# Batch by batch instead of all batches first: where the input norm, the first routing and the filter's hidden layers stand in a two-layer kernel

## What is computed

```python
# layer 0, on normalised tokens x
q, k, v = x @ w_q.T, x @ w_k.T, x @ w_v.T
attn = softmax(causal(rotate(q) @ rotate(k).T / sqrt(128))) @ v      # 4 batches, 1024 x 1024
h = xres + attn
# expert layer 0: 8 experts, capacity 512 each, top-1, routed by xn @ wg
dispatch = one_hot(argmax(logits)) * (place < C)
out0 = combine(gate, dispatch, exp_in @ W[e].T + b)
# layer 1: long convolution; the filter h comes from a small MLP of positions
h = gelu(pos_emb @ W1 + b1); h = gelu(h @ W2 + b2); h = (h @ W3 + b3) * decay
y = ((x @ Wu + bu) * causal_fft_conv(x @ Wv + bv, h)) @ Wo + bo
# expert layer 1: 8 experts, top-2, hidden width 256
```

## Time and profile before

| what | us |
|---|---|
| three runs: median (lowest to highest) | 493.45 (492.63 to 493.60) |
| the profiled execution, whole | 493.04 |
| its span, first to last instruction | 491.2 |
| busy: PE | 366.0 (75%) |
| busy: DVE | 294.4 (60%) |
| busy: POOL | 258.4 (53%) |
| busy: ACT | 225.9 (46%) |

### The profile page before, as it was taken

One profiled execution on the slowest core, in us unless ns is written; L12 is line 12 of the kernel. 1 busy time (PEld: TensorE's weight loads), 2 busy tenths in 40 slices (PEclk: granted clock), 3 DMA queues, 4 the chain that ended last, 5 costly groups with the idle time before them and its releaser, 6 DMA issues.

```text
span 491.2 us, 7805 instructions
## 1 busy us (share of the span) xinstructions
PE 366.0 (75%) x2302; PEld 298.7 (61%) x2302; DVE 294.4 (60%) x782; ACT 225.9 (46%) x551; POOL 258.4 (53%) x254
## 2 busy tenths in 40 slices
PE   2485588869997975949997978898887777766720
PEld 0272255658675644737996867787776667755620
DVE  3977569614773796474688993478438772244105
ACT  1373042325332316334343066434567676687724
POOL 2754766733666323016566676666666555365540
PEclk9999599997998999687998999999999999999975
DMA  9999999823321330001111282445322215422407
GB/s 211 396 197 262 166 140 135 268 51 85 87 75 40 111 89 1 1 5 39 34 34 37 69 261 75 142 140 151 112 69 75 63 29 158 137 74 74 126 11 252
DMA packets 64744, 55.05 MB, mean 112 GB/s; under 512 B 6819, under 2 KB 56683, under 8 KB 64446
## 3 DMA queue, kind: packets, MB, share of 16 engines
q1 hardware_dynamic: 57888, 41.71, 35.6%
q0 software_dynamic: 6656, 12.51, 8.4%
q10 hardware_dynamic: 158, 0.33, 0.4%
HBM read 30.44 MB, written 25.27 MB: 113 GB/s over the span
## 4 chain that ended last, share of the span: by engine, by line
PE 44%; issue 13%; ACT 12%; DVE 10%; DMA 10%; POOL 8%; SPq 1%; ACTq 0%; POOLq 0%; DVEq 0%
PE psS L1161 19%; PE psO L1161 15%; PE psT L1161 7%; ACT hT L1122 7%; POOL slots L826 4%; DMA slots<-row,slot 4%; DMA moe<-ys,xs 2%; POOL w L847 2%; DMA xres<-in_x 2%; ACT row L1027 1%; PE psT L1263 1%; POOL moe L836 1%; DVE work L1713 1%; DVE xres L1747 1%; DMA moe<-ys,ring 1%
## 5 line engine op out<-in xcount | busy, mean ns | idle before, releaser
L813 POOL DMA_INDIRECT slots<-row,slot x64 | 69.3, 1083 | 57.0 <-DVE slot L1580 22.4
L836 POOL DMA_INDIRECT moe<-ys,xs x61 | 61.1, 1001 | 58.3 <-issue 16.6
L1161 PE MATMUL psO<-ring,hT 128*128 128x128 f32 x320 | 45.2, 284 | 45.1 <-ACT hT L1122 45.1
L1161 PEld LDWEIGHTS psO<-ring,hT 128*128 128x128 f32 x320 | 38.7, 191 | 53.4 <-issue 53.4
L1122 ACT ACTIVATE hT<-psT,ring 128x128 f32<-128x128 f32 x160 | 45.6, 368 | 45.7 <-PE psT L1161 45.7
L1868 DVE TENSOR_TENSOR ys<-psO,ring 128x256 f32<-128x256 f32 x40 | 17.0, 424 | 75.3 <-PE psO L1161 75.1
L1055 ACT ACTIVATE ring<-w 128x642 f32 x80 | 55.9, 761 | 1.1 <-issue 1.0
L1161 PE MATMUL psS<-work 128*128 128x512 f32 (+3 forms) x96 | 42.6, 558 | 12.6 <-DVE work L1696 8.8
L836 POOL DMA_INDIRECT moe<-ys,w x35 | 38.0, 1087 | 23.3 <-DVE ys L1868 9.7
L1020 ACT ACTIVATE work<-psT 128x512 f32<-128x512 f32 (+3 forms) x32 | 16.5, 516 | 66.6 <-PE psT L1263 66.6
L826 POOL DMA_INDIRECT slots<-row,slot x32 | 34.9, 1091 | 18.1 <-DMA slots<-row,slot 10.9
(11 more groups left out here) (272 smaller groups left out, 781.4 us busy)
## 6 DMA issues: line engine op xcount, KB each, us to landing
slots<-xs SPq DMA_DIRECT2D x14, 516.0 KB, 14.7
mats<-in_iv SPq DMA_DIRECT2D x16, 256.0 KB, 3.7
xs<-slots SPq DMA_DIRECT2D x61, 64.5 KB, 1.9
w<-in_w SPq DMA_DIRECT2D x8, 321.0 KB
w<-slots SPq DMA_DIRECT2D x35, 64.5 KB, 1.9
xres<-in_x SPq DMA_DIRECT2D x4, 512.0 KB, 9.7
mats<-in_fw SPq DMA_DIRECT2D x1, 2048.0 KB, 11.3
moe<-xs SPq DMA_DIRECT2D x4, 512.0 KB, 7.8
```

Of the source, the lines that this page charges most:

```text
L813: pool.indirect_dma_start(slots1[:, :], bass.IndirectOffsetOnAxis(ap=(slot1, slot2)[k][:, i:i + 1], axis=0), row[:, i, :], None, bounds_ch ...
L836: pool.indirect_dma_start(dst[:, :], bass.IndirectOffsetOnAxis(ap=row_slots[l][m][:, D:ROWW].bitcast(I32), axis=0), ys[:, n % UNROLL, :], ...
L1161: return pe.matmul(o, lhsT, rhs, start=start, stop=stop)
```

## The change

- *Order.* Only batch 0 is normalised, transposed, projected and rotated before row 0. `transpose_tokens(1)` follows `scores(0)`; batches g = 1, 2, 3 get `values_and_gates(g)` in row g - 1, and batches 2 and 3 `transpose_tokens(g)` in row g - 2. DVE normalises batches 0 and 2, ACT batches 1 and 3 (`norm_rows0`, with a bias from `negative_means0`).
- *Filter.* The first hidden layer begins before row 0, its tanh is in row 1, its last polynomial in row 2; the second layer stands in rows 3 to 5. The polynomials leave POOL; DVE does each with one two-input instruction (four in all instead of eight on POOL). The last layer and the spectrum move from rows 2 to 7 to rows 6 to 11, and `filter_layer` uses bank `S[1]` both times.
- *First routing.* Its first six steps are behind row 2 on DVE, the rest at the head of row 3.
- *Later rows.* Expert layer 0 starts in row 12 instead of 8 (`MOE0_FROM`), the split of the biases in row 13 instead of 9; most additions, norms and steps of the second routing move one row later.
- *SP.* q/k weights and rotation tables come ahead of x's later batches; the DFT matrices, the weights of expert layer 0 and the biases come behind the first fill. The weights of layer 1 (2.7 MB) are loaded behind the first 16 sorted tiles instead of ahead of them.

```diff
-FILT_RADIX_AT, FILT_DFT_AT = 3, 6
-SPLIT_AT = 9
-GATES_AT = (24, 25, 29)
-NORM_AT = {23: [(0, 0), (0, 1)], 24: [(1, 0), (1, 1)], 27: [(2, 0)], 28: [(2, 1)]}
-COUNTS_AT = 27
+FILT_HIDDEN_AT, FILT_RADIX_AT, FILT_DFT_AT = 3, 7, 10
+SPLIT_AT = 13
+ROUTING0_AT = 2
+GATES_AT = (25, 26, 29)
+NORM_AT = {24: [(0, 0), (0, 1)], 25: [(1, 0), (1, 1)], 27: [(2, 0)], 28: [(2, 1)]}
+COUNTS_AT = 28
-MOE0_FROM = 8
+MOE0_FROM = 12
-ADD_BEFORE_MAX = {22: (4, 8), 23: (12, 16), 25: (20, 24), 29: (24, 28), 31: (28, 30)}
-ADD_BEHIND_ROW = {21: (0, 4), 22: (8, 12), 24: (16, 20)}
-ROUTING_BEFORE_MAX = {26: 6, 28: 8}
-ROUTING_BEHIND_ROW = {26: 6, 27: 10, 28: R1_STEPS}
+ADD_BEFORE_MAX = {23: (4, 8), 24: (12, 16), 26: (20, 24), 29: (24, 28), 31: (28, 30)}
+ADD_BEHIND_ROW = {22: (0, 4), 23: (8, 12), 25: (16, 20)}
+ROUTING_BEFORE_MAX = {27: 6, 29: 8}
+ROUTING_BEHIND_ROW = {27: 6, 28: 10, 29: R1_STEPS}
...
+def tokens_at(n):
+    return [n + 2] if 0 <= n + 2 < B else []
+def values_at(n):
+    return [n + 1] if 0 <= n + 1 < B else []
...
+            load_x(0)
+            sp.dma_start(cst[:, :], cst_in).then_inc(cst_loaded, 16)
             sp.dma_start(wqk, wqk_in).then_inc(rope_loaded, 16)
+            sp.dma_start(wvg, wvg_in).then_inc(w_a_loaded, 16)
+            load_x(1)
             sp.dma_start(rope, rope_in).then_inc(rope_loaded, 16)
+            load_x(2)
+            load_x(3)
...
 @block.gpsimd
-            inverse_std(0)
-            inverse_std(1)
-            filter_cubic(0)
-            inverse_std(2)
-            inverse_std(3)
-            filter_gelu(0)
-            filter_cubic(1)
-            filter_gelu(1)
+            for g in range(B):
+                inverse_std(g)
...
 @block.scalar
+            take_transposes(0)
+            take_values(0)
+            norm_rows0(1)
+            act.wait_ge(filt_loaded, 32)
+            filter_layer(0)
             exp_rows(0)
+            take_transposes(1)
             for n in range(NT):
                 take_pt(n)
                 if n + 1 < NT:
                     exp_rows(n + 1)
+                for g in values_at(n):
+                    take_values(g)
+                for g in tokens_at(n):
+                    take_transposes(g)
+                if n == 0:
+                    norm_rows0(B - 1)
+                if n == ROUTING0_AT:
+                    routing0_exp()
+                if n == FILT_HIDDEN_AT - 2:
+                    filter_tanh(0)
+                if n == FILT_HIDDEN_AT:
+                    filter_layer(1)
+                if n == FILT_HIDDEN_AT + 1:
+                    filter_tanh(1)
...
 @block.tensor
+            transpose_tokens(0)
+            pe.wait_ge(rope_loaded, 32)
+            pe.wait_ge(tr_free, 1)
+            project(0, 0)
+            pe.wait_ge(w_a_loaded, 16)
+            values_and_gates(0)
             pe.wait_ge(filt_loaded, 32)
             filter_layer(0)
...
             scores(0)
+            transpose_tokens(1)
             for n in range(NT):
                 for b, h in projections_at(n):
                     project(b, h)
                 if n + 1 < NT:
                     scores(n + 1)
+                if n == ROUTING0_AT + 1:
+                    wait_emptied(pe, O_USES, O_AT[("c", 0)])
+                    routing_counts(0, o_bank("c", 0))
+                if n == FILT_HIDDEN_AT:
+                    filter_layer(1)
                 transpose_probs(n)
...
                 if n:
                     weigh_values(n - 1)
+                for g in values_at(n):
+                    values_and_gates(g)
+                for g in tokens_at(n):
+                    transpose_tokens(g)
...
 @block.vector
+            norm_stats(0)
+            norm_rows(0)
+            norm_stats(1)
             dve.wait_ge(rope_loaded, 32)
             rotate(0, 0)
+            negative_means0(1)
+            norm_stats(2)
+            row_max(0)
+            norm_stats(3)
+            norm_rows(2)
...
+                if n == ROUTING0_AT + 1:
+                    finish(first_layer_routing)
+                if n == FILT_HIDDEN_AT - 1:
+                    filter_gelu(0)
+                if n == FILT_HIDDEN_AT + 1:
+                    filter_cubic(1)
+                if n == FILT_HIDDEN_AT + 2:
+                    filter_gelu(1)
...
+                if n == 0:
+                    negative_means0(B - 1)
+                    filter_cubic(0)
+                if n == ROUTING0_AT:
+                    dve.wait_ge(cst_loaded, 16)
+                    dve.wait_ge(vg_free, 4 * B)
+                    take(first_layer_routing, R0_OH)
```

More of the change, by code:

```diff
@@ L526, in two_layer_kernel @@
         issued = sem("issued")
-        T_USES, O_USES = [], []
+        T_USES = [("xt", u) for u in range(4)]
+        O_USES = [("vg", u) for u in range(4)]
         for n in range(NT):
+            if n == ROUTING0_AT + 1:
+                O_USES.append(("c", 0))
             T_USES += [("p", n, c) for c in range((n % J + 4) // 4)]
@@ L538, in two_layer_kernel @@
                 O_USES.append(("o", n - 1))
+            O_USES += [("vg", 4 * g + u) for g in values_at(n) for u in range(4)]
+            T_USES += [("xt", 2 * g + u) for g in tokens_at(n) for u in range(2)]
             T_USES += [("x", e) for e in expert0_at(n)]
@@ L729, in _ @@
             for n in range(TILES0):
+                if n == UNROLL:
+                    sp.wait_ge(rad_f, RAD_F)
                 load_rows(0, slots0, n)
+                if n == RING[0] - 1:
+                    for a, b in [(w12[:, e, :], w12_in[e]) for e in range(E)] + [
+                            (wv[:, :], wv_in), (wu[:, :], wu_in), (wg1[:, :], wg1_in), (wo[:, :], wo_in)]:
+                        sp.dma_start(a, b).then_inc(l1_w_loaded, 16)
             for m in range(RING[0]):
@@ L952, in take_values, with norm_rows0 @@
                                    ACT.Copy).then_inc(vg_free, 1)
+            def norm_rows0(g):
+                act.wait_ge(neg0_done, g // 2 + 1)
+                for i in range(J * g, J * g + J):
+                    act.activation(row[:, i, 0:D], xres[:, i, :], ACT.Identity, bias=nbias[:, i:i + 1],
+                                   scale=rstd[:, i:i + 1]).then_inc(xn0_act, 1)
             def filter_layer(k):
                 act.wait_ge(f_full, k + 1)
-                act.activation(hx[0:FO, :], S[k][0:FO, :, :].rearrange("p a m -> p (a m)"), ACT.Identity,
+                act.activation(hx[0:FO, :], S[1][0:FO, :, :].rearrange("p a m -> p (a m)"), ACT.Identity,
                                bias=(f1b, f2b)[k], scale=(1.0, 0.5)[k]).then_inc(f_act, 1)
@@ L1491, in norm_rows, with negative_means0, filter_cubic, filter_gelu @@
                     ts(row[:, i, 0:D], xres[:, i, :], mv[:, i, 0:1], rstd[:, i:i + 1], ALU.subtract,
-                       ALU.mult).then_inc(xn_done, 1)
-            def norms(k0):
-                norm_stats(k0)
-                for k in range(k0 + 1, k0 + B):
-                    norm_stats(k)
-                    norm_rows(k - 1)
-                norm_rows(k0 + B - 1)
+                       ALU.mult).then_inc(xn0_dve if k < B else xn_done, 1)
+            def negative_means0(g):
+                tiles = slice(J * g, J * g + J)
+                dve.wait_ge(rstd_done, J * (g + 1))
+                stt(nbias[:, tiles], mv[:, tiles, 0], -1.0, rstd[:, tiles], ALU.mult, ALU.mult).then_inc(neg0_done, 1)
+            def filter_cubic(k):
+                dve.wait_ge(f_act, 3 * k + 2)
+                stt(ht[0:FO, :], ht[0:FO, :], 1.0, hx[0:FO, :], ALU.add, ALU.mult).then_inc(f_dve, 1)
+            def filter_gelu(k):
+                dve.wait_ge(f_act, 3 * k + 3)
+                stt(hg[0:FO, :], hg[0:FO, :], 1.0, hx[0:FO, :], ALU.add, ALU.mult).then_inc(f_dve, 1)
             n_rt = [0]
@@ L1539, in routing0 @@
                 yield from inverse_sum(None, NT, gate0[:, :])
-                yield from earlier_tokens(0, None, NT, O[0])
+                yield from earlier_tokens(0, None, NT, o_bank("c", 0))
                 assert n_rt[0] == R0_CUM
```

127 lines of the change are left out of this document (45 added, 82 removed).

## The result

The changed kernel takes **500.76 us** (median of four, 500.17 to 501.10) against 493.04 us (491.58 to 493.60) for the kernel before on the same chip: ratio 1.016, 95% interval 1.0134 to 1.0185. The profiled execution took 500.60 us for a span of 498.5, 7.3 us more than the 491.2 before. The forecast was 498.4 us, slower.

The account below looks back on a forecast made before the run. One chain of scatter, send-back, additions, routing and second scatter, headed by `slot0`, was taken to bound the kernel. 7.2 + 2.3 - 1.0 - 2.9 - 0.6 = +5.0 on 493.45 gives 498.4 us; own range 495.5 to 502, with rivals 489.5 to 503.5.

Parts of the forecast that it names:

- Part 1: Start of row 0: `scores(0)` needs only the rotation tables, comes at about 23.5, row 0 some 30 us earlier.
- Part 2: Start of the first scatter: gates wait behind ScalarE's list of rows 0 to 2; first issue 60.1 against 52.84, +7.2.
- Part 3: Scatter to additions: TensorE waits some 5 us in row 12; second expert falls in a projection row, +2.3.
- idle time in row 12: Sign in row 12: TensorE idle for a sorted tile until 113 to 119; no idle time would show the forecast wrong.
- The supply of the send-back: GpSimd's send-back of expert results: second expert comes in row 14, a projection row of 8.65 against 6.1, +2.3.
- Part 4: First addition to second slots, 46.1 before: one attention row fewer, but routing and exponential behind other work, -1.0.
- Part 5: Second scatter: GpSimd's 2.87 wait for the last tiles' statistics goes, -2.9, and a slack is used up, -0.6.
- the slack of 0.6: At 281, TensorE taking the first tiles of the second experts: the slack is used up, -0.6.
- The shorter tail: Rival: the whole projection row leaves the stretch from additions to second slots, -8.65 for -1.0, 490.8 us; chance 0.24.
- The rival of no waits in the first rows: First rows' lists run without waits: scatter at 53.5, 493.4 us, the change does nothing; chance 0.11.
- The rival of late early rows: ScalarE's waits twice as long, rows 4 to 12 no quicker: scatter at 65, +10, 503 us; chance 0.08.
- VectorE's polynomials did hold up GpSimd's issues: Rival, first scatter: an issue held for VectorE's 1.2 us, twice, +2.4, 500.8 us; chance 0.07.

Follow-up runs that it names:

- the run with the other order: Changed kernel with the last 20 steps of the first routing ahead of the additions of tiles 24 to 27: 500.69 us, ratio 1.0178.

## Why the prediction was right, and where not

The direction and the size came out, and the first-order reason with them: the start of the scatter moved by what I had forecast. Ahead of row 12 and ahead of the second experts, however, something else ended last than I had written, and the total is as near as it is because errors cancelled.

**Part 1** was right in its mechanism. The rotation tables were there at 14.1 (forecast 15), `scores(0)` came at 24.82 (23.5). The projection took 6.65 us where I had put the 3.60 of the earlier trace rows.

**Part 2**, the term that decides, came out: the gates' last copy ended at 51.6 (51.2), six steps took 2.9 (2.9), the rest 4.8 (4.8), the first issue came at 60.48 (60.1): +7.6 for +7.2. The 51.6 is in part luck: ScalarE's list began at 21.2 (19.0), its work was 22.6 us (25.6) and its idle time 7.7 (6.6), and these errors cancel. Its wait behind the polynomial in row 2 was 1.70 (2.0). My upper bound was added up wrongly: twice the waits gives 66.7, not 66.

The two drawn-out instructions of the earlier trace rows are gone (0.42 for 2.07, 0.18 for 1.69) as GpSimd's polynomials are. I had called their removal worth nothing to the chain, and yet took these 3.2 us out of the routing for it; that GpSimd was idle for 29.89 us ahead of the first issue shows only that nobody waited for it. Its size is seen in the kernel before, where it starts the scatter 8.8 us sooner, at 44.07. Both that kernel and the changed one have the polynomials on VectorE, so the new order, with all that it brings, costs 16.4 us at the start of the scatter, of which the polynomials pay back about half.

What GpSimd's polynomials did to VectorE's norm tiles is gone too: the longest of them now takes 379 ns where one took 2505.

```profile
L1516 DVE TENSOR_SCALAR row<-xres,mv,rstd x24: 315/344/379, 10.2 to 248.7; 128x128 f32<-128x128 f32 x24
```

**Part 3** is the step that failed in its mechanism. I had TensorE in row 12 at 111 and idle for 5 us until 116.1. It came at 115.48 and waited 0.34, until 116.31: the tile was on time, TensorE was 4.5 us late. Of that, 1.3 was there at `scores(0)`; its rows ahead of 12 then took 90.7 us (87.5 forecast, with the waits of the first rows in it). The chain of waits of the changed kernel, 54 to 124 us (start us, us, what), has no scatter in it:

```profile
55.36 3.60 PE psS L1183 x4
...
105.17 3.57 PE psT L1183 x32
...
114.17 1.20 DVE work L1722 x2
...
120.80 0.44 PE psT L1317 x4
```

One of the causes can be read off: the spectrum's first 32 products took 5.44 us at 97.70 (3.81 in the kernel before), the next 3.74 at 105.01, with the granted clock at 0.86 and 0.80 in the two stretches from 95 to 105, behind waits of 1.15, 1.92 and 0.89 us. The rest of the 3.2 us isn't split up. So my sentence that the experts' move from row 8 to 12 "neither helps nor hurts while the scatter is later than the row" had its condition on the edge. The send-back still began near its forecast, and that is luck: scatter and TensorE ended within about a microsecond of each other. In the kernel before a later scatter alone gives 500.4, and in the changed one, with the start of the scatter taken 1 us sooner but TensorE 5.3 later, the time is 505.0. The "idle time in row 12", my own test, came out wrong. First send-back +6.3, for +7.2.

The supply of the send-back was +3.2 (50.4 against 47.2) for +2.3. It stands where I put it, at the second expert, as the 2.79 us ahead of the third pair; with the experts in row 11 this wait is absent.

**Part 4** was -0.5 (45.55 against 46.07) for -1.0. The terms that I had written down, 4 us less and 2.1 and 1.6 more, add up to -0.3 and not to -1.0. Two runs split it: with the routing ahead of the additions this stretch took 44.2, so their order costs 1.4 (2.1 forecast); with the row numbers of before it took 46.6. The second slots were then 8.4 late, for 8.5. This agreement too is a sum of errors: +7.6 at the scatter, -1.3 to the first send-back, +3.2 in the send-back, -0.6 to the first addition and -0.5 here, for +7.2, 0, +2.3, 0 and -1.0.

**Part 5** was mis-sized. The wait of 2.87 became 0.53, -2.3 for -2.9, and the slack of 0.6 was not used up but grew: the loads were issued 6.6 late, the first tile was taken 7.2 late. TensorE's prelude began 6.2 late and took 43.9 us instead of 42.9, its granted clock at 0.50 in 270 to 275 (before: 0.66 in 265 to 270). I had written that the prelude moves by the same amount as the scatter and then counted -0.6; it is the second branch that ended last, as the run with the other order shows. Together -1.2 where I had -3.5: that is the 2.3 us between +5.0 and +7.3.

**The rivals.** The shorter tail (490.8) didn't happen; the stretch got 0.5 us shorter and not 8.65. The rival of no waits in the first rows (scatter at 53.5) is excluded by 60.48. The rival of late early rows (scatter at 65) didn't come either, though TensorE was later than forecast. VectorE's polynomials did hold up GpSimd's issues, by less than its price of 2.4: the two issues beside them (68.08 and 73.34) took 1.45 and 1.61 us instead of 0.97, 1.1 in all; the first had a rotation sum beside it as well. The scatter as a whole was shorter all the same, 31 intervals in 50.1 us against 51.8, and with TensorE at row 12 only 0.34 us ahead of the tile little of this could reach the end. That the rival's 500.8 is the measured number is chance.

## What to carry over

Work moved ahead of a chain helps only if the head of the chain comes sooner, so follow the one value that starts it (here `slot0`) through the in-order lists and write down what now stands ahead of it. Where two engines meet within a microsecond or two of each other, neither's profile row alone tells the gain: taking time from one showed 0.3 to 1.9 us here, delaying one cost 4.5 of 5.3 us of span. Of this change the part worth keeping is the smallest: the polynomials on VectorE with the weights' loads behind the first loads of slots, and the rows left as they were, took 486.6 and 487.7 us against 493.5 and 493.4, ratios 0.983 and 0.988.

## What the runs showed of the hardware

- TensorE's first work ran at about half pace in both kernels although the profile's clock column says 1.00. In the changed kernel eight products of 512 columns took 6.65 us at 14.10 and 3.70 at 62.46; in the kernel before the eight token transposes at 14.17 took 2.21 and those at 30.29 took 1.04. The Trainium skill (page "TensorE: Matmul & The Clock Gate", section "What's actually happening") says that "the default state is throttled, and activity releases the throttle"; the pace in the rows agrees, the clock column of that stretch (us from to, length, busy, granted clock, DMA share, GB/s) doesn't show it:

```profile
15.00:20.00 5.00, 5.00 (x7) 1.00 1.22 252
```

  The projection that the change moved to the front paid for it: 6.65 us for 3.60.
- GpSimd paused ahead of the 29th indirect issue in each timeline of the first scatter: 2.1 us in the changed kernel and in the one before, 4.29 and 2.13 in two executions of one kernel, 8.10 where the loads of the weights and the fills kept the DMA engines busy. Most pairs of issues took 3.02 us in all of them. What the pause is, no run here shows.
- VectorE and GpSimd hold each other up, in both directions. With GpSimd's polynomials gone, VectorE's drawn-out instructions are gone (0.42 us for 2.07); with three more of them, the rotation's sums took 3.42 us for 1.28; and beside VectorE's polynomials an indirect issue took 1.61 us for 0.97. In the kernel before, the issues of over 1.2 us behind the first one (six, up to 1.93) all have a rotation sum or a radix step of the filter beside them. This agrees with the port rule that the prediction takes from the Trainium skill (page "SBUF — State Buffer", section "SBUF: two separate sides").
- A clock that falls in the wrong 5 us cost 2.95 us in one round, once, in a kernel that differed little from one where it didn't.
